# Latent attention on one core: values of two key tiles together, at most four row transfers under way, late key buffers cleared by ScalarE

## What is computed

```python
x = x + hybrid(_layernorm(x), ...)          # Mamba (256 channels, 16 states), then the experts
x = x + _L0_ffn_ref(_layernorm(x), w_gate, w_up, w_down)      # hidden 384, silu gate
x = x + _L0_attn_b_ref(_layernorm(x), W_dq, W_uq, W_dkv, W_uk, W_uv, W_o)
x = x + _L0_ffn_ref(_layernorm(x), w_gate, w_up, w_down)
```

```python
k_eff = (W_dq.T @ W_uq.T @ W_uk).reshape(nh, hs, n_kvl)     # nh = 16 heads, hs = 8
v_eff = jnp.transpose((W_uv.T @ W_o.T).reshape(n_kvl, nh, hs), (1, 0, 2))
c_kv = x @ W_dkv.T
q = (x @ W_dq.T @ W_uq.T).reshape(B, T, nh, hs)
q_lat = jnp.einsum('bqhd,hdl->bhql', q, k_eff)
attn = jnp.einsum('bhql,bkl->bhqk', q_lat, c_kv) / sqrt(hs)
attn = jax.nn.softmax(jnp.where(causal, attn, -jnp.inf), axis=-1)
y = jnp.einsum('bhql,hld->bqhd', jnp.einsum('bhqk,bkl->bhql', attn, c_kv), v_eff)
```

## Time and profile before

| what | value |
|---|---|
| median of 3 runs | 755.37 us (752.66 to 756.16) |
| the profiled execution: its own time, its span | 755.38 us, 753.6 us |
| TensorE matmuls | 611.8 us busy (81%), 3556 |
| TensorE weight loads | 364.9 us (48%), 3575 |
| VectorE | 517.9 us (69%), 1339 |
| ScalarE | 390.0 us (52%), 626 |
| GpSimd | 332.1 us (44%), 295 |
| transfers | 31676 packets, 32.10 MB, 43 GB/s in the mean |
| chain that ended last | TensorE 43%, VectorE 6%, ScalarE 3%, issue 3%, transfers 2% |

### The profile page before, as it was taken

How to read it: one execution, slowest core, us unless ns; L and a number is a source line. 1 busy time by engine, 2 the same in 40 slices (tenths; PEclk the granted TensorE clock), 3 DMA queues, 4 the chain that set the end, 5 groups by cost and what they waited for, 6 DMA issues and landing times.

```text
span 753.6 us, 11260 instructions
## 1 busy us (share of the span) xinstructions
PE 611.8 (81%) x3556; PEld 364.9 (48%) x3575; DVE 517.9 (69%) x1339; ACT 390.0 (52%) x626; POOL 332.1 (44%) x295
## 2 busy tenths in 40 slices
PE   1966887888177778778999999946899699998897
PEld 1422333344022223378999888923544344544454
DVE  6679999956999799744533735387587487885052
ACT  1546667533356456356767656402266365566721
POOL 5229989800579999322678323344012012111010
PEclk9978999999589899989999999967999899999999
DMA  5700000000500000030123201522505204000001
GB/s 153 252 0 2 0 0 1 0 0 28 196 18 18 19 4 0 1 86 19 43 83 88 78 16 34 99 75 41 69 3 70 37 3 83 21 3 2 1 15 43
DMA packets 31676, 32.10 MB, mean 43 GB/s; under 512 B 5394, under 2 KB 26914, under 8 KB 31362
## 3 DMA queue, kind: packets, MB, share of 16 engines
q1 hardware_dynamic: 26274, 25.45, 14.2%
q0 software_dynamic: 2496, 5.15, 2.0%
q10 hardware_dynamic: 2848, 0.78, 0.5%
HBM read 13.90 MB, written 9.25 MB: 31 GB/s over the span
## 4 chain that ended last, share of the span: by engine, by line
PE 43%; DVE 6%; ACT 3%; issue 3%; DMA 2%; ACTq 1%; POOL 0%; DVEq 0%; POOLq 0%
PE ps L1467 40%; DVE arena L1389 3%; ACT arena L1002 2%; DMA arena<-arena 2%; PE ps L1753 1%; ACTq L994 1%; PE ps L1643 1%; DVE stats L1085 1%; DVE x L1329 1%; PE ps L1760 1%; DVE nb L1098 0%; ACT arena L991 0%; ACT arena L1010 0%; DMA arena<-moe_rows 0%; DVE mv L1088 0%
## 5 line engine op out<-in xcount | busy, mean ns | idle before, releaser
L1467 PE MATMUL ps<-arena 128*128 128x128 f32 (+12 forms) x2427 | 378.2, 341 | 69.0 <-DVE arena L1389 17.2
L1467 PEld LDWEIGHTS ps<-arena 128*128 128x128 f32 (+4 forms) x2446 | 221.9, 151 | 192.6 <-issue 77.1
L1467 PE MATMUL ps<-arena,ident 128*128 128x512 f32 x256 | 133.7, 655 | 40.4 <-DVE arena L1265 40.4
L1255 DVE TENSOR_TENSOR_SCAN arena<-ps,arena 128x512 f32<-128x512 f32 x128 | 147.5, 1202 | 8.1 <-POOL arena L769 6.0
L1389 DVE CUSTOM_DVE_ANT_0 arena<-ps,cmask 128x128 f32<-128x128 f32 (+3 forms) x256 | 115.1, 516 | 30.9 <-PE ps L1467 24.4
L769 POOL TENSOR_TENSOR arena<-arena 128x1024 f32<-128x1024 f32 x64 | 127.8, 2014 | 5.6 <-ACT arena L933 5.0
L942 ACT ACTIVATE ps<-arena 128x512 f32<-128x512 f32 x128 | 88.4, 694 | 60.1 <-DVE arena L1255 59.8
L1002 ACT ACTIVATE arena<-ps 128x1024 f32<-128x1024 f32 (+3 forms) x128 | 84.9, 709 | 58.5 <-PE ps L1467 56.3
L1467 PEld LDWEIGHTS ps<-arena,ident 128*128 128x128 f32 x256 | 50.3, 206 | 102.1 <-DVE arena L1265 56.6
L1441 DVE TENSOR_TENSOR arena<-arena,ps 128x512 f32<-128x512 f32 x46 | 31.7, 688 | 73.7 <-PE ps L1467 58.2
L754 POOL DMA_INDIRECT moe_out<-arena,xT x46 | 44.8, 974 | 73.4 <-DVE arena L1413 60.0
(11 more groups left out here) (181 smaller groups left out, 610.2 us busy)
## 6 DMA issues: line engine op xcount, KB each, us to landing
arena<-arena SPq DMA_DIRECT2D x120, 64.0 KB
moe_rows<-arena SPq DMA_DIRECT2D x2, 1495.0 KB, 11.8
arena<-moe_rows SPq DMA_DIRECT2D x8, 325.0 KB, 5.0
arena<-in_L_attn_a_Wg SPq DMA_DIRECT2D x1, 2048.0 KB, 8.5
arena<-in_L_attn_a_Wu SPq DMA_DIRECT2D x1, 2048.0 KB, 13.5
arena<-moe_out SPq DMA_DIRECT2D x4, 512.0 KB, 4.7
x<-n_L_attn_a_hidden_states SPq DMA_DIRECT2D x4, 256.0 KB, 4.9
out<-x SPq DMA_DIRECT2D x4, 256.0 KB, 2.3
```

The source lines that it names most:

```text
L1255: V.tensor_tensor_scan(hst[:, g % STATES, e, :], bank(6 + e), dBx[:, g % RING, e, :], 0.0, ALU.mult, ALU.add).then_inc(s_scan, 1)
L1467: return T.matmul(o, l, rr, start=start, stop=stop)
```

## The change

It has three parts.

1. **Values in pairs.** A third buffer of exponentials is laid over `r`, memory that the experts used; `pts` holds the three. `PATTERN` puts the values of units c − 2 and c − 1 behind each other in the half of the even unit, ahead of the last group of maxima, and none in the half of the odd unit; the last two values stand together at the end. `exps` waits for the values of unit c − 2 in place of c − 1, and once, at unit 2, for VectorE to have read `r`.
2. **Four transfers under way.** `place` counts its placements over all batches (`sent`) and has two semaphores for queries and two for keys, even and odd. Before a placement goes out, SyncE waits until the one two back has landed: at most two placements of the same kind, four transfers, are under way. Whoever waited for all 28 now waits on both semaphores (`all_rows`).
3. **Clears.** `clear_keys(1)` and `clear_keys(2)` go from GpSimd's memset to a copy of a zero row by ScalarE: the first between the last expert block and the rest of the steps, the second in the step `combine` of the last batch.

```diff
         junk = carve([2, L])
+        pts = (pt[:, 0], pt[:, 1], r[:, :, :].rearrange("p (g k) d -> p g (k d)", g=4))
         fh0 = vv[:, NB - 1].rearrange("p t h w -> p (t h w)")[:, 0:HT * L].rearrange("p (f l) -> p f l", f=HT)
...
         s_qp = sem("parts_ready")
-        s_qk = [[sem(f"{w}_rows_placed{b}") for w in "qk"] for b in range(NB)]
+        s_qk = [[sem(f"{w}_rows_placed_{g}") for g in range(2)] for w in "qk"]
         s_qz = [sem(f"q_zeros_placed{b}") for b in range(NB)]
...
                 eng.wait_ge(s, n)
+
+        def all_rows(eng, b, w):
+
+            for g in range(2):
+                eng.wait_ge(s_qk[w][g], 32 * ((7 * b + 8 - g) // 2))
...
-        PATTERN = (("maxima", 0, "use", "maxima", 1, "maxima", "values", "short"),
-                   (0, "use", "maxima", 1, "maxima", "values", "short"))
+        PATTERN = (("maxima", 0, "use", "maxima", 1, "values", "maxima", "short"),
+                   (0, "use", "maxima", 1, "maxima", "short"))
         ramp = {(1, 1): [("combine", 2), ("f_norm", 0, 2)], (2, 0): [("f_normalise", 0, 2), ("f_turn", 0, 2)],
...
                     elif part == "values":
-                        if 0 < c <= NB * UNITS:
-                            steps.append(("values", c - 1))
+                        if 2 <= c <= NB * UNITS:
+                            steps += [("values", c - 2), ("values", c - 1)]
                             if c % UNITS == 0:
...
                 later = [None, ("place_max", b, j // HP)] + later
-        steps.append(("values", NB * UNITS - 1))
+        for c in range(NB * UNITS - 2, NB * UNITS):
+            steps.append(("values", c))
         steps += use
...
                   43: [("f_down", 1)], 44: [("f_add", 1)]}
-        ramp_first = steps[:steps.index(("qk_rest", 1, 0))]
         tile_after = {30: (0, 0), 31: (0, 1), 32: (0, 2), 34: (1, 0), 35: (1, 1), 36: (1, 2)}
...
                 g = kslot(b) if w else b % SL
+                sent = 7 * b + (0 if 0 in parts else 3)
                 for n, part in enumerate(((0, 0, 1, 0, 2, 1, 1), (0, 1, 0, 2, 0, 1, 2))[w]):
                     if part in parts:
+                        landed = s_qk[w][sent % 2]
+                        if sent > 1:
+                            sp.wait_ge(landed, 32 * (sent // 2))
+                        sent += 1
                         for r in range(2):
...
                             sp.dma_start(kz[rows, g, r, :, :] if w else qq[rows, g, :, :],
-                                         qp[64 * r:64 * r + 64, w, part, :]).then_inc(s_qk[b][w], 16)
+                                         qp[64 * r:64 * r + 64, w, part, :]).then_inc(landed, 16)
...
                 if b:
-                    pool.wait_ge(s_qk[b - 1][w], 16 * 14)
+                    all_rows(pool, b - 1, w)
                 G.tensor_copy(qp[:, w, 1, :], qr[:, w, :]).then_inc(s_qp, 1)
...
             clear_values(NB - 1)
-            pool.wait_ge(s_u2, NITEM)
-            clear_keys(1)
-            attend(parts, ramp_first)
-            pool.wait_ge(s_cb, NB)
-            clear_keys(2)
-            attend(parts, steps[len(ramp_first):] + last_ffn)
+            attend(parts, steps + last_ffn)
...
             S.preload_act_table(ACT.Silu)
+            def clear_keys(b):
+                S.copy(kz[:, kslot(b), :, :, :].rearrange("p r j l -> p (r j l)").bitcast(F32).rearrange(
+                    "p (n l) -> p n l", l=L // 2),
+                       zeror[:, :].bitcast(F32).unsqueeze(1).to_broadcast([P, 2 * PAIRS, L // 2])).then_inc(s_kz, 1)
+
+            def clear_last(b):
+                if b == NB - 1:
+                    act.wait_ge(s_cb, NB)
+                    clear_keys(2)
+
             def turn(b):
...
                 if b:
-                    act.wait_ge(s_qk[b - 1][w], 16 * 14)
+                    all_rows(act, b - 1, w)
                 S.copy(qp[:, w, 0, :], bank(7)).then_inc(s_qh, 1)
...
                 if q == 0:
-                    wait(act, s_pv, c - 1)
+                    wait(act, s_pv, c - 2)
+                    if c == 2:
+                        act.wait_ge(s_xr, NB)
                 act.wait_ge(s_s2, 2 * c + q + 1)
-                S.activation(pt[:, c % 2, 2 * q:2 * q + 2, kt * P:L], ps[:, 2 * q:2 * q + 2, kt * P:L],
+                S.activation(pts[c % 3][:, 2 * q:2 * q + 2, kt * P:L], ps[:, 2 * q:2 * q + 2, kt * P:L],
                              ACT.Exp).then_inc(s_ex, 1)
...
                     attend(parts, in_moe.get(i, []))
+            parts["combine"] = clear_last
+            act.wait_ge(s_u2, NITEM)
+            act.wait_ge(s_kz, 1)
+            clear_keys(1)
             attend(parts, steps)
...
                     for w in range(2):
-                        pe.wait_ge(s_qk[b][w], 16 * 14)
+                        all_rows(pe, b, w)
                     pe.wait_ge(s_qz[b], 32)
...
                     last = mm(ps[32 * g:32 * g + 32, 6, kt * P:L], vv[:, b, kt, 4 * u + g, :],
-                              pt[:, c % 2, g, kt * P:L], start=(kt == 0), stop=(kt == TB - 1))
+                              pts[c % 3][:, g, kt * P:L], start=(kt == 0), stop=(kt == TB - 1))
                 last.then_inc(s_pv, 1)
```

## The result

The changed kernel takes 763.82 us (median of 4 runs, 762.67 to 764.3), the kernel before beside it 754.93: ratio 1.0106, 95% interval 1.0079 to 1.0133. The forecast was 737.9 with a range to 749.

A forecast was written before the change was run, and what follows sets the result against it. The prediction took TensorE as the bound, busy 152.1 of 171 us in the attention stage. Its terms, −2.7 + 0.3 − 1.5 − 7.3 − 2.0 + 2.2 − 5.0 − 1.5 = −17.5, took 755.4 to 737.9 us; range 729 to 749.

The forecast's parts named there:

- The pace of the limited queue: SyncE's row transfers: 1.7 us a placement, between 1.31 and 1.98, so a batch is done 24.7 us after first issue.
- batch 3: Wait for this batch's rows: TensorE waits 4.7 us, +2.2 us against before, ends −2.5 and +5.8.
- Batch 0 at +0.3: First maxima at 490.98 us: the limit moves them by −1 to +2 us, taken as +0.3.
- The gain at batch 2: TensorE's hole at 581 to 597 us: falls from 6.3 to 1.8 us; with clock, short waits and switches −7.3.
- Turns between queues: Rival at the 581 to 597 us hole: it stays at 6.3 us with the lower clock; 744 us, chance 0.08.
- The clears: Ramp: two VectorE maxima no longer held beside GpSimd's memsets, 1.5 and 1.2 us, −2.7 in all (0 to 4.8).
- The terms of part 1: Values in pairs, attention stretches 546–581, 597–622, 645.7–689 and 689–717 us: −1.5, −2.0, −5.0 and −1.5 us.
- The price of a switch: TensorE leaving and re-entering full-width form for values: 0.19 us a round trip, 24 fewer, 4.6 us saved.
- the overlap: Around moved values and the third maxima group: TensorE's waits for late exponentials and VectorE expected to shrink; no separate size.
- the cover of these terms: VectorE's slack in the attention carries the gains from paired values; without it they fall to a half, 5 us in all.
- The −5.0: Stretch 645.7–689 us: 6.5 switches (1.2 us) and 3.5 us of idle plus tails saved; VectorE needs 35.1 of 43.3.
- the limit starves the queue: Rival on row transfers: only one pair moves at a time, 17.3 us of wait for batch 3; 764 us, chance 0.04.

The follow-up runs named there:

- clears_only: Only the key buffer clears moved from GpSimd's memset to ScalarE, against the kernel before: ratio 0.9982 (0.9960 to 1.0004).
- the balanced pairs: Kernel before with third buffer and paired values, one group of maxima moved from the even to the odd unit's half: ratio 1.0041 against before.

## Why the prediction was wrong

The forecast for the profiled execution was −17.5 us, and +7.3 came. By its own steps:

- **The pace of the limited queue** failed. I took P = 1.7 us a placement between 1.31 (issue) and 1.98 (backlog), with the sentence that "a batch ends 2.57 + 13 P after its first issue". Measured is a cycle of 4.2 us for two placements, P = 2.1, above my upper end, and 31.5 us for a batch in place of 24.7. Two assumptions were false. The landing of a lone pair was read from its last packet (2.57); the wait ends at 3.85. And the backlog's pace was taken as the slowest that a queue can have, though a limit adds the completion to every cycle. This is most of the 6.6 us missed at batch 3 (8.8 measured against 2.2).
- **Batch 0 at +0.3** failed by the same number. Its maxima start right when the rows land, as I wrote, so 7 us more for a batch go to the first maxima: 5.8 measured. At unit 0 3.6 to 5.1 of them are left without the clears' help (85.1 and 85.5 us of ramp against 80.4 to 81.5), and the limit for batch 0 alone makes the kernel 0.74% slower, 5.6 us.
- **The gain at batch 2** held. −7.3 forecast, −8.8 measured; TensorE no longer waits for a transfer there, where I had 1.8 left. Turns between queues, by which the limit would win nothing, are out: the limit for batch 2 alone wins 0.85%, and with its transfers out of the way the hole goes. With six allowed 0.5 us of it is left. So the transfers ahead of the maxima's were the cause. How they hold it the packets narrow down: before, the maxima's two transfers are issued from 581.09 on and their 30 packets start between 589.04 and 590.42; in the changed kernel they are issued from 585.85 on and the packets start between 587.22 and 588.17. Once begun they take 1.0 to 1.4 us either way; the delay stands ahead of the first packet. The rule that I quoted from the Trainium skill (DMA: Bandwidth & Descriptors, Queues, rings and completion order), turns between the queues with work, does not give these delays as I read it, since it is no slow taking of turns that is seen but a late start; the measurement decides. What the packets wait for before they start no run shows.
- **The clears** held in sign and, alone, about in size. −2.7 was forecast, as 1.5 and 1.2; alone they are worth about 3 us (3.4 by the ramps of the traces, 1.4 to 4.1 by the runs), in the changed kernel about 1 (84.2 us of ramp against 85.1 and 85.5), so behind the late rows of batch 0 there is less to win. The two terms were off in opposite ways, and their sum is near by luck: behind the maximum at 495.52 the next one starts 2.90 us later, where `clears_only` has 0.61 between the same two, so the first memset cost 2.3, with 0.73 of waiting for TensorE in it that I left out; behind the second the step is 0.86 in place of 0.20, a cost of 0.7.
- **The terms of part 1** failed: −1.5, −2.0, −5.0 and −1.5 for +1.8, +0.8, +1.3 and −0.1, 13.8 us together. The price of a switch was right in kind: 24 of 0.19 are 4.6 us, and the windows show 3 to 4 us less of TensorE's work in four fifths of the units. What failed is the overlap: of the waits around the moved values and the third group of maxima behind them I wrote "These waits are what I expect to shrink", and they grew, from 1.3 to 5.8 us for VectorE's maxima in the three windows. I looked at what TensorE waits for now and not at what the move takes from VectorE. Values are TensorE's work in which VectorE catches up, once in each half; put together ahead of a group of maxima they starve it in one half and leave it no time in the other. That is how the timeline of one wait reads; the sums of the waits speak for it, and so do the two orders without a group of maxima behind the pair, in which the attention's loss is gone. I had VectorE's slack as "the cover of these terms", priced its loss at half of them, and never below nothing. The +1.3 in units 36 to 48 isn't the pairs' own: alone they take 29.9 there, as before. It comes behind the wait for batch 3, with the granted clock at 0.96. The −5.0 forecast there is missed all the same.

The rival *the limit starves the queue* gave 764 and is nearest in time, and the measured P of 2.1 to 2.2 lies below the 2.4 from which it was to decide. Its batch was 37 us and its wait for batch 3 17 us, against 31.5 and 9.3, and its wait of 7.7 us at batch 2 did not come. That its time is near is luck: the pairs' loss, which it did not have, filled the rest.

What stays open: why the third buffer alone, the pairs behind the maxima and the balanced pairs measure 0.2 to 0.4% slower as whole kernels, when their attention is within 0.6 us of before; and whether a balanced order of pairs gains at all. Among maxima its windows say 1.8 us, the whole kernels don't show it.

## What to carry to other kernels

In these runs a tight limit on transfers under way gave others a quick passage and slowed its own batch: before setting one, ask for each batch how long after its issue it is needed, and limit only those with time to spare. Price a wait on a transfer by when the waiting engine goes on, not by the last packet. Before moving one engine's work together, look at which second engine uses the gaps between its pieces: where it is nearly as busy (here 77 to 83% of the time), evenly spread work can be worth more than fewer switches.

## What the runs showed of the hardware

- Two transfers of 12 KB issued by ScalarE at 581.09 us, behind nine of SyncE's, started their first packet 7.95 us later; with at most four of SyncE's under way, 1.37 us later.
- The wait on a placement's semaphore ended 1.3 us after its last packet (packets through in 2.56 us, wait over at 3.85 from the first issue).
- A limit of one, two and three placements gave batches of 50, 28 to 29 and 22 to 25 us from first to last issue (33 and 30 where the parts came late), no limit 18.6 to 21 (26 where the parts came late). A limit of three left 0.5 us of the 6.3 us hole and made the kernel 0.7% faster.
- ScalarE's copy of 128 x 4096 f32 from a repeated zero row takes 3.61 us, as long as GpSimd's memset (3.54). Beside the memsets two maxima took 2.17 and 1.91 us, with the copy in the memset's place the same forms took 0.69 and 0.55.
- The granted clock was 0.81 over the 20.5 us with the hole of 9.3 us and 0.96 over the 31 us behind it; the four matmuls behind the hole took 1.44 us for 0.82.
